# Two engine assignments changed in a mixture-of-experts stage, and the first loads of an attention layer split up, in a four-stage transformer kernel

## What is computed

```
x = x + attention0(layernorm(x))      # 16 heads of 16, causal
x = x + mixture(layernorm(x))         # 8 experts, top 2 for each (token, output), dense expert matmuls
x = x + attention1(layernorm(x))      # 16 query heads of 128, 4 key/value heads
x = x + mlp(layernorm(x))             # fp4 weights, GELU, width 2048

# mixture:
logits = (h @ router_w.T + router_b).reshape(T, O, E)
probs  = softmax(logits);  w, sel = top_k(probs, 2);  w = w / sum(w)
c      = zeros((T, E)).at[t, sel].add(w)              # token weights
final  = einsum('te,teo->to', c, einsum('th,eoh->teo', h, expert_w) + expert_b)
```

## Time and profile before

| | |
|---|---|
| median of 3 runs | 1146.77 us (1146.24 to 1148.51) |
| profiled execution | 1145.4 us, of which the span from first to last instruction is 1143.7 us |
| busy share of the span | PE 86%, DVE 75%, ACT 43%, POOL 28% |
| mean granted TensorE clock | 0.946 of full speed |
| start, layer 0 attention, mixture | 0 to 48, 48 to 286, 286 to 614 us |

### The profile page before, as it was taken

One profiled execution on the slowest core, in us unless ns is written; L12 is line 12 of the kernel. 1 busy time (PEld: TensorE's weight loads), 2 busy tenths in 40 slices (PEclk: granted clock), 3 DMA queues, 4 the chain that ended last, 5 costly groups with the idle time before them and its releaser, 6 DMA issues. The chain is left out here.

```text
span 1143.7 us, 19971 instructions
## 1 busy us (share of the span) xinstructions
PE 985.4 (86%) x6960; PEld 578.7 (51%) x6960; DVE 852.3 (75%) x1556; ACT 496.9 (43%) x972; POOL 315.1 (28%) x341
## 2 busy tenths in 40 slices
PE   2698989897789869697778899999978999999997
PEld 1344545454445435354334466574846556656564
DVE  5677777750999999999998875858653776777766
ACT  2054444454466364645543523426131444444443
POOL 3234343451262423432550221304054300000000
PEclk9799999998989989888879999999979999999999
DMA  6722222200101001001000000101011000000000
GB/s 177 119 76 75 75 76 74 75 1 1 48 0 47 1 1 46 0 0 47 1 0 20 19 21 10 29 1 37 3 38 44 13 1 19 1 18 0 19 1 19
DMA packets 37087, 35.87 MB, mean 31 GB/s; under 512 B 8584, under 2 KB 33416, under 8 KB 37008
## 3 DMA queue, kind: packets, MB, share of 16 engines
q1 hardware_dynamic: 35728, 33.79, 10.3%
q10 hardware_dynamic: 1280, 1.05, 0.7%
HBM read 27.28 MB, written 6.29 MB: 29 GB/s over the span
## 5 line engine op out<-in xcount | busy, mean ns | idle before, releaser
L893 DVE TENSOR_REDUCE bm<-ps 128x4 f32<-128x512 f32 x160 | 102.1, 684 | 32.5 <-PE ps L613 30.3
L792 ACT ACTIVATE pt<-ps 128x1024 f32<-128x1024 f32 (+1 forms) x96 | 82.0, 881 | 71.1 <-PE ps L689 70.5
L2105 ACT ACTIVATE g<-ps 128x512 f32<-128x512 f32 x64 | 38.2, 596 | 136.4 <-PE ps L2052 109.9
L2155 DVE SCALAR_TENSOR_TENSOR g<-g,ps 128x512 f32<-128x512 f32 x64 | 43.9, 687 | 54.7 <-ACT g L2105 54.4
L609 PE MATMUL ps<-ks,qs 96*128 96x512 bf16 (+3 forms) x256 | 68.4, 322 | 12.1 <-DMA ks<-scratch_k 7.8
L165 POOL TENSOR_TENSOR mag_w<-stage 128x512 f32<-128x512 fp8e4 x24 | 26.4, 1099 | 184.3 <-DVE stage L152 184.3
L557 POOL TENSOR_SCALAR_AFFINE_SELECT pt<-pt 128x256 f32<-128x256 f32 (+1 forms) x96 | 45.8, 483 | 110.3 <-ACT pt L792 109.7
L1604 PE MATMUL ps<-wp_hi,oT_hi 128*128 128x256 bf16 x256 | 71.0, 277 | 5.6 <-DVE oT_lo L1837 5.4
L2068 PE MATMUL ps<-ew_hi,it_hi 128*128 128x256 bf16 x256 | 70.0, 274 | 6.2 <-DVE it_lo L2171 6.1
L1604 PE MATMUL ps<-wp_lo,oT_hi 128*128 128x256 bf16 x256 | 70.9, 277 | 0.0
L1604 PE MATMUL ps<-wp_hi,oT_lo 128*128 128x256 bf16 x256 | 70.8, 277 | 0.0
(11 more groups left out here) (290 smaller groups left out, 2817.5 us busy)
## 6 DMA issues: line engine op xcount, KB each, us to landing
qs<-scratch_q SPq DMA_DIRECT2D x64, 64.0 KB, 2.6
ks<-scratch_k SPq DMA_DIRECT2D x48, 64.0 KB, 2.6
q_next<-in_w_qkv SPq DMA_DIRECT2D x4, 768.0 KB, 4.4
X<-in_x SPq DMA_DIRECT2D x4, 512.0 KB, 6.9
w_next<-in_router_w SPq DMA_DIRECT2D x4, 512.0 KB, 3.8
w_next<-in_expert_w SPq DMA_DIRECT2D x4, 512.0 KB, 4.6
p_next<-in_w_proj SPq DMA_DIRECT2D x4, 512.0 KB, 5.4
out<-X SPq DMA_DIRECT2D x8, 256.0 KB, 2.3
```

The source lines that it names most:

```text
L792: act.activation(pt[kt][:, heads[0]:heads[-1] + 1, :], src, ACT.Exp).then_inc(s_exp, 1)
L893: ins = dve.tensor_reduce(bm[:, 2 * g + i // 5, 4 * (i % 5):4 * (i % 5) + 4], src.rearrange("p (k q) -> p k q", k=4), AX_X, ALU.max)
```

## The change

There are three parts.

1. **Mixture.** The low part `xb_lo` of each tile goes from GpSimd to VectorE (new `tile_low` in VectorE's list, behind `weigh`, for tile n+2). `xb_hi` on ScalarE now stands behind the logits of the same tile. In exchange the layernorm of the next batch goes from VectorE (4 instructions) to ScalarE (8 instructions, in t = 1, ahead of the logits): first x − mean, then times rstd. GpSimd makes −mean for it, 4 columns.
2. **Start, GpSimd.** The fills wait for `wsplit_lo`.
3. **Start, loads.** The first half's four scratch writes each have a semaphore (`s_first`) and no longer wait for each other; SP loads the eight stacks of group 0 part by part as they land, keys too. ScalarE's queue issues the key stacks of groups 1 to 3. `queries_keys` waits chunk by chunk, in all batches.

```diff
+        s_first = [st.sem(f"first_part{k}") for k in range(4)]
...
+        def stack_part(eng, g, n, part):
+            heads = slice(HG * g, HG * (g + 1))
+            scr, dst, hi_lo_rows = ((scratch_q, qs, ((0, 2), (1, 3))), (scratch_k, ks, ((0, 1), (2, 3))))[n]
+            for r in hi_lo_rows[part]:
+                eng.dma_start(dst[HD0 * r:HD0 * (r + 1), heads, :],
+                              scr[part].rearrange("(h d) t -> d h t", d=HD0)[:, heads, :]).then_inc(s_stk[g], 16)
...
-                for half_ in range(2):
-                    copy_parts(0, [START.index(("qk", m)) for m in range(4)], half_)
-                    wait_alone(sp, s_scr[half_], 64, passed_sp)
-                    for g in (2 * half_, 2 * half_ + 1):
-                        stack_rows(sp, g, (0,))
+                for k in range(4):
+                    n, part = divmod(k, 2)
+                    if part:
+                        sp.wait_ge(s_taken, START.index(("qk", 2 * n)) + 1)
+                    else:
+                        sp.wait_ge(s_qkhi, n + 1)
+                    sp.dma_start((scratch_q, scratch_k)[n][part, 0:P, :], (qk_hi, qk_lo)[part][:, 2 * n, :]
+                                 ).then_inc(s_first[k], 16)
+                for k in range(4):
+                    wait_alone(sp, s_first[k], 16, passed_sp)
+                    n, part = divmod(k, 2)
+                    stack_part(sp, 0, n, part)
+                sp.sem_inc(s_scr[0], 64)
+                stack_rows(sp, 1, (0,))
+                copy_parts(0, [START.index(("qk", m)) for m in range(4)], 1)
+                wait_alone(sp, s_scr[1], 64, passed_sp)
+                for g in (2, 3):
+                    stack_rows(sp, g, (0,))
...
                 root(0)
-                pool.wait_ge(s_rstd, 2)
+                wait_alone(pool, wsplit_lo, 1, passed_pool)
                 pool.memset(ones4[:, :], 0.0).then_inc(s_ties, 1)
...
                     for c in range(KC):
+                        if arrived is not None:
+                            pe.wait_ge(s_xhi, arrived + c + 1)
+                            pe.wait_ge(s_xlo, arrived + c + 1)
...
-                    pe.wait_ge(s_xhi, 2 * b + 2)
-                    pe.wait_ge(s_xlo, 2 * b + 2)
...
                         if t == 0 and not last:
                             rstd_ops(pool, mv, rstd, half, s_mv, s_rstd, b + 1, passed_pool)
+                            pool.tensor_scalar(minus_mean[:, :], mv[:, :, 0], -1.0, None, ALU.mult).then_inc(s_neg, 1)
...
+                def normalised(b):
+                    act.wait_ge(s_rstd, 2 * b + 2)
+                    act.wait_ge(s_neg, b)
+                    for j in range(4):
+                        act.activation(xn[:, j, :], X[:, b, j, :], ACT.Identity, bias=minus_mean[:, j:j + 1]
+                                       ).then_inc(s_centred, 1)
+                    for j in range(4):
+                        act.wait_ge(s_centred, 4 * (b - 1) + j + 1)
+                        act.activation(xn[:, j, :], xn[:, j, :], ACT.Copy, scale=rstd[:, j:j + 1]).then_inc(s_xn, 1)
...
+                def tile_low(n, t):
+                    dve.wait_ge(s_xbhi, n + 1)
+                    dve.tensor_tensor(xb_lo[t % 2][:, :, :], xf[:, :, P * t:P * (t + 1)], xb_hi[t % 2][:, :, :],
+                                      ALU.subtract).then_inc(s_xblo, 1)
...
                         weigh(b, n, t)
+                        if routed:
+                            tile_low(n + 2, routed[1])
```

More of the change, by code:

```diff
@@ L387, in all_batches @@
             batch(B - 1, False, True)
+        def stack_part(eng, g, n, part):
[4 more added lines that the diff above has]
+                              scr[part].rearrange("(h d) t -> d h t", d=HD0)[:, heads, :]).then_inc(s_stk[g], 16)
         def stack_rows(eng, g, which):
-            heads = slice(HG * g, HG * (g + 1))
             for n in which:
[L393 to L397, removed]
+                for part in range(2):
+                    stack_part(eng, g, n, part)
         with nc.Block() as block:
@@ L567, in _, with three @@
                 pe.wait_ge(const, 4)
-                def three(out, lhs, rhs):
+                def three(out, lhs, rhs, arrived=None):
                     n = 0
                     for c in range(KC):
+                        if arrived is not None:
+                            pe.wait_ge(s_xhi, arrived + c + 1)
+                            pe.wait_ge(s_xlo, arrived + c + 1)
                         for a, b_ in ((0, 0), (0, 1), (1, 0)):
@@ L778, in _ @@
                     act.wait_ge(s_scr[half_], 64)
-                    for g in (2 * half_, 2 * half_ + 1):
+                    for g in (2 * half_, 2 * half_ + 1)[1 - half_:]:
                         stack_rows(act, g, (1,))
@@ L1040, in _ @@
                 pool.sem_inc(s_rstd, 2)
[L1042 to L1046, removed]
                 def from_middle(n, t):
@@ L1074, in _ @@
                 pool.wait_ge(const, 1)
-                tile_low(0, 0)
                 from_middle(0, 0)
@@ L1079, in batch @@
                     for t, n, after, _ in tiles(b, last):
-                        if after and t != 2:
-                            tile_low(n + 1, after[1])
                         if after:
@@ L1238, in _ @@
                 tile_high(0, 0, 0)
+                tile_high(0, 1, 1)
                 logits(1, 1)
@@ L1244, in batch @@
                     for t, n, after, routed in tiles(b, last):
-                        if after and t < 2:
-                            tile_high(after[0], n + 1, after[1])
-                        if t == 3 and not last:
-                            tile_high(after[0], n + 1, after[1])
+                        if t == 1 and not last:
+                            normalised(b + 1)
                         if routed:
                             logits(n + 2, routed[1])
-                        if t == 1:
-                            tile_high(b, n + 2, 3)
+                            tile_high(routed[0], n + 2, routed[1])
                         if last and t == 2:
@@ L1283, in _ @@
                 dve.sem_inc(s_mv, 4)
-                dve.sem_inc(s_xn, 4)
                 dve.sem_inc(s_xlo, 2)
@@ L1420, in _ @@
                 two_greatest(0, 0)
+                tile_low(0, 0)
+                tile_low(1, 1)
                 from_second(0, 0)
@@ L1425, in batch @@
                 def batch(b, first, last):
-                    for t, n, after, _ in tiles(b, last):
-                        if t == 1 and not last:
-                            normalised(b + 1)
+                    for t, n, after, routed in tiles(b, last):
                         if t == 2 and not last:
```

12 lines of the change are left out of this document (4 added, 8 removed).

## The result

The changed kernel takes **1136.59 us** (median of 4 runs, 1135.01 to 1137.41) against 1147.64 us (1146.24 to 1151.71) for the kernel before, timed together: ratio 0.9896, 95% interval 0.9868 to 0.9925. The prediction was 1136.9 us, with a range of 1132 to 1142. The profiled execution took 1136.15 us, with a span of 1134.4.

A forecast was written before the change was run, and what follows sets the result against it. Bounds taken: a chain of single steps at the start, PE busiest in the layer 0 loop, VectorE's list in the mixture. Start −5.9, loop −1.0 and mixture −3.0 sum to −9.9 us, giving 1136.9 us, range 1132.0 to 1142.0.

The forecast's parts named there:

- Start: Kernel start: later fills, chunk waits and part-by-part loads bring the first scores 5.9 us sooner, bounds −7 and −4.3.
- the rival of loads that stay as they were: Start: group 0's loads still land with the median 5.0 us or more; start −3.5, 1139.3 us in all; chance 0.12.
- Chunks in the loop: Layer 0 loop: chunk-by-chunk waits save 0.3 us in each of three batches, −1.0 us, bounds 0 and −2.
- Mixture: Mixture: moving `xn` and `xb_lo` between engines shortens VectorE's list, −3.0 us in all, bounds +1 and −6.
- The first period: Mixture's first period, batch 0: entered in the sum as −1.4 us, with a t = 1 wait of 1.6 us.
- the stretching of VectorE's instructions: Mixture: GpSimd's `xb_lo` lengthens VectorE instructions running at the same time; removing it saves about 1.5 us per period.
- In the other passes ScalarE is ready 3 us or more before: Mixture, passes other than t = 1: ScalarE finishes `xb_hi` 3 us or more early, so VectorE's `xb_lo` does not wait.
- the 0.5 us that I had given back for the root: Mixture: 0.5 us allowed for GpSimd's root slowing VectorE, turning −3.5 into −3.0 us.
- The rival in which it blocks: Mixture: root blocks VectorE's tournament (2.2 us more) or ScalarE's `xn` takes 4 us or more; 1140.9 us; joint chance 0.17.
- Slower: Mixture t = 1: ScalarE's `xn` makes VectorE wait over 3.6 us more per batch, cancelling the 9.9 us; chance 0.03.
- a start that gives only −2.3: Start: the fills were not what stretched `xn`, so the start gives −2.3 us; stated as 1143.3 us; chance 0.03.

The follow-up runs named there:

- the fills alone: Kernel before with only GpSimd's fills held back until the weight split: 1143.24 us, ratio 0.9965.
- the loads with the chunks: Kernel before with group 0's writes and loads part by part, its keys on SP and chunk-by-chunk waits, fills untouched: 1146.15 us, ratio 0.9981.
- The half experiments: Kernel before, mixture only: `xb_lo` to VectorE with `xb_hi` behind the logits, 1149.84 us; or only `xn` to ScalarE, 1143.78 us.
- late split: Changed kernel with ScalarE's weight split (`wq_hi`, `wp_hi`) moved from the end of t = 0 to t = 1: 1135.9 us, again 1132.9 us.
- the mixture-alone kernel: Kernel before with only the mixture's part of the change: 1144.28 us, ratio 0.9961.

## Why the prediction was right, point by point

**Start (−5.9 expected, −5.28 measured).** `xn` went from 4.94 to 1.38 us, exactly as priced. The root came 0.4 us later in this execution, which explains `qk_hi` at 17.04 instead of 16.5 and 0.4 of the 1.35 us by which the maxima (26.95) miss 25.6. The rest of that miss is in the second `qk_hi` (19.02, 2.0 us behind the first instead of 1.3), since TensorE kept its slow pitch longer than before, and in a landing of 2.9 instead of 2.6 us. Over several runs the forecast holds. Kernels with the old start have their first scores at 48.01, 49.26, 48.73 and 49.01, mean 48.75; six executions with the new start at 42.73, 43.71, 43.18, 42.41, 43.18 and 42.56, mean 42.96: −5.8 us. Against that mean the fills alone give 3.6 us and the loads with the chunks 1.9. Both act; the rival of loads that stay as they were is out. What the chunks give of it is not shown: TensorE begins 0.8 us sooner with them alone, but the first scores of that run, 48.94, are no sooner than the mean.

**Chunks in the loop (−1.0, measured −1.18).** The sum agrees, the cause isn't shown. Five executions with the old loop took 238.68 to 240.35 us, mean 239.6; eight with the chunks 234.57 to 240.85, mean 238.6. The difference equals the forecast, but one kernel's loop scatters by more than that, and the two runs that add the chunks to the mixture of before took 239.04 and 240.85 us. This step stays open.

**Mixture (−3.0, measured −2.80; −3.06 alone).** Four executions with the old mixture took 326.98 to 327.62 us, three with the new one 324.41 to 324.74, so the gain is well clear of the scatter. The head grew 0.91 us (0.9 expected). The wait in t = 1 was 1.10 us (0.9), and in batch 0, 1.77 (1.6) behind 2.52 in t = 0 (2.4). The eight `xn` start 0.40 us apart and take 3.2 us, the value that I had taken from the token weights. The half experiments price the other terms. `xb_lo` on VectorE with its stretching of other instructions gone is worth about 0.2 us per period: the 1.36 put in and the 1.5 taken out nearly cancel, as in the sum. `xn` with its wait gone is worth 2.16, 1.80 and 1.53 us per period, less than 2.23, because `masked` then waits for the sigmoid (0.83, 1.10 and 1.38 us per period, of which 0.5 to 0.6 come back since fewer of VectorE's instructions are stretched).

Two terms of the sum were wrong and hid each other. The first period stands in it with −1.4, but a gain of 2.4 less a wait of 1.6 is 0.8; written so, the mixture would have been −2.4. And the stretching of VectorE's instructions was read in batch 1 alone, where it is 1.6 us (about 1.5 in the text). In the first period of the kernel before it is 3.6 us, in the third 2.3, since there GpSimd's `wt` also runs into `from_second`, as in the timeline of that kernel:

```profile
352.84 4.58 POOL L1053 TENSOR_TENSOR wt<-lg,tourney 128x2048 f32<-128x2048 f32 x1 [11.23 <-DVE tourney L1337]
...
356.34 3.23 DVE L1343 TENSOR_TENSOR far<-lg,tourney 128x2048 f32<-128x2048 f32 x1
```

After the change 0.7, 0 and 0.7 us of it are left. So the first period gained 1.33 us although VectorE waited 2.67 us in it. That it came near the −1.4 is luck.

**One step failed.** "In the other passes ScalarE is ready 3 us or more before": in t = 2 it wasn't, since I followed only ScalarE's own list. `xn` holds up the logits, these hold up the transposes (TensorE waits 1.31 us for them), and so the router of t = 2. The waits were 0.33 and 0.43 us in batches 1 and 2, and 0.90 in batch 0. That is 1.7 us in all. The room was small from the start: in the kernel before, ScalarE's last logits of that pass end 30.4 us after `masked` and VectorE is through `weigh` at 33.0; in the changed kernel VectorE is there at 31.1, and the router's first matmul moved from +21.2 to +21.9. Three things covered the 1.7 us: the 0.5 us that I had given back for the root was not needed, the stretching that went in the first period was 1.5 us more than priced, and the list gains a little more than 2.4 us. With the late split, where neither t = 1 nor t = 2 waits, the periods are 2.72, 2.63 and 2.60 us under those of before, 0.2 to 0.3 more each.

**The root.** The rival in which it blocks is refuted: the tournament beside it takes 1.22 us in each execution that I looked at, not 2.1. By the Trainium skill, page "SBUF — State Buffer", section "SBUF: two separate sides", the two should shut each other out for a whole instruction. The traces agree for the large cases, whose numbers follow. At the head of the mixture GpSimd's 4.63 us subtraction holds up one `xb_lo` of 0.42 us to 4.83 (changed kernel, timeline):

```profile
287.55 5.17 DVE L1314 TENSOR_TENSOR xb_lo<-xf,xb_hi 128x256 bf16<-128x256 f32 x2
...
287.81 4.63 POOL L1067 TENSOR_TENSOR wt<-first_lg,tourney 128x2048 f32<-128x2048 f32 x1 [8.12 <-DVE tourney L1354]
```

and the root itself, 1.05 us at the kernel's start, takes 2.95 when it starts during `masked`. But VectorE lost nothing when it began the tournament (393.48) 1 us before the root ended (394.46). The measurement decides: for this pair there is no price.

**Slower.** Nothing spoke for it. Half of the change is slower by itself, though: the low part on VectorE costs 1.8 us of mixture, at its two ends (0.9 and 1.5) and not in the periods (−0.6). Together the parts give −2.80 where the halves add up to 1.77 − 4.63 = −2.86; the agreement is chance, for neither the periods (−4.05 together, −0.61 − 5.49 apart) nor the two ends add.

**The median.** 1136.59 against 1136.9 is nearer than the steps are, and that is luck. The profiled execution of the kernel before, 1145.4 us, is as fast as the fastest of 33 later runs of it (1145.34, median 1147.35). Timed together the change gave 11.05 us, and 13.1 when both were timed again, where the forecast was 9.9 and the landmarks of two executions give 9.3. The rest is of the size of the scatter in the stages where TensorE is busiest; which part of the change it would belong to is not shown. In the list of rivals, a start that gives only −2.3 makes −6.3 in all and 1140.5 us, not 1143.3, so that rival lay inside the range; and 9.9 us over three batches are 3.3 us each, not the 3.6 of the case *Slower*.

## What to carry to other kernels

Price a step in the engine's list that bounds the stage, but then follow the results of the moved instructions through every engine to the next pass. Here the moved `xn` cost 4.0 us of waits in t = 1, which the list of ScalarE foretold, and 1.7 us in t = 2, which only the chain over the transposes and the router shows. And read the stretching of instructions that run side by side in every batch, not in one. If a moved step must wait on something in its new list, look first for work ahead of it that nobody needs yet: moving two weight copies one pass later gave 3.6 to 3.9 us of the mixture, more than the whole exchange of engines did. Where one kernel's runs scatter by more than the gain, compare landmarks of a stage rather than whole times.

## What the runs showed of the hardware

**The same code runs at another clock from run to run.** The start of the kernel before and of the mixture-alone kernel is one and the same code. In the first the 128 x 512 matmuls turn from 0.43 us apart (512 columns, the 1.2 GHz level) to 0.215 us apart (2.4 GHz) by 21.08. In the second they are slow until about 22.5, some 1.7 us longer; in both TensorE had worked without a gap since 18.2 to 18.3. The timeline of the second:

```profile
21.15 0.63 PE L574 MATMUL ps<-xT_lo,first_lg 128*128 128x512 bf16 x1
22.43 0.49 PE L574 MATMUL ps<-xT_lo,first_lg 128*128 128x512 bf16 x1
22.76 0.60 PE L574 MATMUL ps<-xT_hi,first_lg 128*128 128x512 bf16 x2
23.19 0.38 PE L574 MATMUL ps<-xT_lo,first_lg 128*128 128x512 bf16 x1
```

With it the second to fourth products, the writes and the loads come later: the first scores at 49.26 instead of 48.01. The new start has its first fast `xT_lo` matmul at 18.39 in one execution and 20.43 in another. The clock column of the windows view (third from the right) reads 1.00 over such a stretch, here 19 to 21 us of the second execution, with matmuls 0.43 us apart, so the pitch has to be read instead:

```profile
19.00:21.00 2.00, 2.00 (x6) 0.73 (x5) 0.00 (x0) 0.03 (x1) 0.00 (x0) 1.00 0.00 0
```

**The long stages scatter too.** The late-split kernel was profiled twice. Its loop and its rest by the windows view, in the first execution:

```profile
43.18:283.92 240.74, 214.40 (x1629) 116.94 (x1629) 145.69 (x334) 112.07 (x152) 96.74 (x149) 0.94 0.17 54
...
605.03:1138.20 533.17, 493.66 (x4102) 310.99 (x4102) 371.85 (x711) 204.00 (x367) 85.16 (x107) 0.97 0.06 17
```

and in the second:

```profile
42.41:276.98 234.57, 206.54 (x1623) 112.03 (x1629) 145.62 (x335) 111.57 (x152) 96.40 (x149) 0.97 0.18 56
...
597.83:1127.00 529.17, 485.92 (x4056) 310.11 (x4102) 371.49 (x711) 203.87 (x367) 85.09 (x107) 0.98 0.07 17
```

VectorE, ScalarE and GpSimd are busy for the same time in both; only TensorE isn't, with a granted clock of 0.94 against 0.97 in the loop (some of its records are missing in the second trace, 4056 of 4102 in the rest). 6.2 us of loop and 4.0 us of rest go with it, in code that is the same. The two executions ran on two chips, but one chip scatters as well: the six runs that belong to the first execution took 1129.43 us (mean granted clock 0.950) to 1139.88 us (0.939). In both stretches TensorE is busy for about nine tenths of the time. The mixture, bound by VectorE, repeats within 0.3 us here (321.11 and 320.85) and within 0.7 us in the kernel before. Over 12 runs this kernel spreads from 1128.7 to 1139.88 us, mean 1134.5; the changed kernel over 8 runs from 1133.39 to 1137.74, mean 1135.7. That the late split gains is therefore shown for the mixture only, not for the whole time; why its other stages scatter more is open.
